# Softmax maxima transposed by VectorE instead of TensorE, first and last stages reordered, in an attention-and-experts kernel

## What is computed

```python
# attention: q from layernorm(x), k and v from the context
wq = (q @ wq_w.T + wq_b).reshape(b, t, H, DH)     # H = 16, DH = 16
wk = (k @ wk_w.T + wk_b).reshape(b, t, H, DH)
wv = (v @ wv_w.T + wv_b).reshape(b, t, H, DH)
scores = einsum('bthd,bshd->bhts', wq, wk) / sqrt(DH)
probs = softmax(scores, axis=-1)
x = x + einsum('bhts,bshd->bthd', probs, wv).reshape(b, t, d) @ wo_w.T + wo_b
# experts: xt = layernorm(x), xhat = layernorm(xt)
top1 = argmax(xt @ Wg.T, axis=-1)                 # 8 experts
for e in experts:
    h = gelu((xhat * ln_scale[e] + ln_bias[e]) @ W1[e] + b1[e])
    y += (top1 == e) * (h @ W2[e] + b2[e])
x = x + y
```

## Time and profile before

| | us |
|---|---|
| median of 3 runs | 1424.43 (1423.45 to 1425.28) |
| profiled execution, device time | 1425.39 |
| profiled execution, span from first to last instruction | 1423.6 |

### The profile page before, as it was taken

How to read it: one execution, slowest core, us unless ns; L and a number is a source line. 1 busy time by engine, 2 the same in 40 slices (tenths; PEclk the granted TensorE clock), 3 DMA queues, 4 the chain that set the end, 5 groups by cost and what they waited for, 6 DMA issues and landing times.

```text
span 1423.6 us, 40094 instructions
## 1 busy us (share of the span) xinstructions
PE 1380.6 (97%) x15314; PEld 1196.9 (84%) x15314; DVE 1158.0 (81%) x2760; ACT 985.6 (69%) x1664; POOL 482.8 (34%) x662
## 2 busy tenths in 40 slices
PE   6899999999999999999999999988999999999998
PEld 5688888888888888888888888876888888888887
DVE  4688888888888888888888888876787878878776
ACT  5477777777777777777777777756667666676764
POOL 4222332233322332233223332324444444444430
PEclk8899999999999999999999999999999999999999
DMA  6656665567656665667566755643343434434322
GB/s 183 144 146 184 171 185 150 159 172 178 161 150 175 174 176 151 167 174 182 154 159 168 185 152 154 167 114 105 91 126 106 127 105 120 117 108 132 102 80 75
DMA packets 168870, 207.46 MB, mean 146 GB/s; under 512 B 19895, under 2 KB 119530, under 8 KB 168682
## 3 DMA queue, kind: packets, MB, share of 16 engines
q1 hardware_dynamic: 168682, 204.89, 54.2%
HBM read 69.26 MB, written 33.81 MB: 72 GB/s over the span
## 4 chain that ended last, share of the span: by engine, by line
PE 88%; DVE 6%; ACT 2%; issue 2%; DMA 1%; POOL 0%; SPq 0%; ACTq 0%; DVEq 0%; POOLq 0%
PE s_ps L1345 13%; PE pp_ps L1219 11%; PE st_ps L1153 8%; PE pv_ps L1167 8%; PE s_ps L1125 8%; PE pp_ps L1192 7%; PE pp_ps L1227 6%; PE st_ps L1370 6%; PE pp_ps L1370 6%; PE pv_ps L1175 4%; PE pp_ps L1213 3%; DVE negmax L830 2%; PE pp_ps L1309 2%; PE t_ps L1144 2%; PE t_ps L1320 1%
## 5 line engine op out<-in xcount | busy, mean ns | idle before, releaser
L644 ACT ACTIVATE pT<-st_ps 128x1024 f32<-128x1024 f32 x256 | 263.1, 1028 | 108.0 <-PE st_ps L1153 107.1
L830 DVE TENSOR_REDUCE negmax<-s_ps 128x8 f32<-128x1024 f32 x256 | 311.2, 1215 | 24.3 <-PE s_ps L1125 24.0
L501 POOL TENSOR_TENSOR q_parts<-q,q_parts 128x1024 bf16<-128x1024 f32 x32 | 68.5, 2141 | 403.3 <-ACT q_parts L638 403.3
L700 ACT ACTIVATE pT<-s_ps,c 128x512 f32<-128x512 f32 x128 | 87.8, 688 | 119.4 <-PE s_ps L1345 114.3
L1125 PE MATMUL s_ps<-k_packed,q_packed 96*128 96x128 bf16 x2048 | 158.0, 220 | 11.2 <-DVE negmax L830 5.8
L1345 PE MATMUL s_ps<-k_packed,w_hi 128*128 128x512 f32 x512 | 165.8, 415 | 0.0
L1153 PE MATMUL st_ps<-q_packed,k_packed 98*128 98x128 bf16 x2048 | 158.1, 220 | 1.5 <-DMA q_packed<-negmaxT 1.5
L1125 PEld LDWEIGHTS s_ps<-k_packed,q_packed 96*128 96x128 bf16 x2048 | 128.1, 98 | 29.7 <-DVE negmax L830 17.5
L1153 PEld LDWEIGHTS st_ps<-q_packed,k_packed 98*128 98x128 bf16 x2048 | 120.6, 98 | 27.3 <-issue 25.0
L513 POOL TENSOR_TENSOR xb<-xin,bo_all 128x256 f32<-128x256 f32 x128 | 90.4, 728 | 150.8 <-DMA x_scratch<-xb 133.1
L1167 PE MATMUL pv_ps<-pT,v 128*32 128x128 f32 x4096 | 138.7, 276 | 0.0
(11 more groups left out here) (199 smaller groups left out, 3679.1 us busy)
## 6 DMA issues: line engine op xcount, KB each, us to landing
q_packed<-q_parts SPq DMA_DIRECT2D x192, 256.0 KB, 4.3
k_packed<-k_parts SPq DMA_DIRECT2D x192, 256.0 KB, 4.6
xin<-in_x_dram SPq DMA_DIRECT2D x32, 512.0 KB, 3.9
cin<-in_ctx_dram SPq DMA_DIRECT2D x32, 512.0 KB, 4.6
out_dram<-xb SPq DMA_DIRECT2D x32, 512.0 KB, 3.2
x_scratch<-xb SPq DMA_DIRECT2D x32, 256.0 KB, 4.8
x_scratch<-xb SPq DMA_DIRECT2D x64, 128.0 KB, 4.7
k_parts<-mask_scratch SPq DMA_DIRECT2D x32, 256.0 KB, 4.0
```

Of the source, the lines that this page charges most:

```text
L644: a.activation(pT[u % 2][:], st_ps[:], ACT.Exp, scale=DH ** -0.5).then_inc(s_exp, 1)
L700: a.activation(hidden32[m], h_ps[m % 2], ACT.Gelu, bias=c1[:, m:m + 1]).then_inc(f_he, 1)
L830: v.tensor_reduce(own, s_ps[:].rearrange("p (h s) -> p h s", s=P), AX_X, ALU.max, negate=True).then_inc(s_red, 1)
```

## The change

**Maxima.** `turn_max` on PE, `keep_max` on ACT and the widened tiles go. Their place takes one DVE instruction a batch, `v.transpose` of the 128x32 bf16 tile of high and low parts, which transposes each 32x32 square by itself. It waits for the low part to be complete, and stands in `maxima` of the batch's second unit. What was one 32x128 tile is now four 32x32 squares, one on each 32 partitions, so `load_max` issues four DMAs of 2 KB for a batch. Before, it was one of 8 KB.

**Start.** PE runs 80 products of a tile of ones before the first weights; VectorE makes that tile, which GpSimd made before. Group 0 is packed in two halves of two batches, 24 DMAs in place of 12, and the first scores wait for the first half alone. The products for the experts' bias move behind `scores(0, 2)`; scores of units 0 to 2 move ahead, between the first items of group 1; statistics of group 2, batch 0, move into group 0; `load_x(2)` moves behind the first `load_max`.

**Last attention group and first experts.** Groups 0 and 3 of the experts are normalised by ACT or at another place; group 0's moves from DVE (unit 1) to ACT (units 1 and 2). GpSimd computes the shift for every group. PE's first experts' group is reordered: `hidden(0, 2)` earlier, `gate(1)` and `turn_logits(1)` later, behind parts of `outputs`. DVE's order follows.

```diff
-        negmax_wide = [sb(f"negmax_wide{n}", [P, P], BF16) for n in range(2)]
-        negmaxT = [sb(f"negmaxT{n}", [2 * H, P], BF16) for n in range(2)]
+        negmax_hl = [sb(f"negmax_hl{n}", [P, 2 * H], BF16) for n in range(2)]
+        negmaxT = [sb(f"negmaxT{n}", [P, 2 * H], BF16) for n in range(2)]
...
+            def pack_half(z, part, half):
+                tok = slice(half * 2 * T, (half + 1) * 2 * T)
...
             def load_max(n, b):
-                sp.wait_ge(s_mte, at(PAIRS, n, b + 1))
-                sp.dma_start(packed[0][n % 2][KP:KP + 2, :, b * T:(b + 1) * T], negmaxT[b % 2][:]).then_inc(ld_mx[b % 2], 16)
+                sp.wait_ge(s_mt, at(PAIRS, n, b + 1))
+                for q in range(P // (2 * H)):
+                    strip = slice(q * 2 * H, (q + 1) * 2 * H)
+                    sp.dma_start(packed[0][n % 2][KP:KP + 2, :, b * T + q * 2 * H:b * T + (q + 1) * 2 * H],
+                                 negmaxT[b % 2][strip, :]).then_inc(ld_mx[b % 2], 16)
...
-            for part in range(3):
-                for z in range(2):
-                    pack(0, z, part)
+            for half in range(2):
+                for part in range(3):
+                    for z in range(2):
+                        pack_half(z, part, half)
+            load_max(0, 0)
             load_x(2)
-            load_max(0, 0)
...
-            def keep_max(n, b):
-
-                act.wait_ge(s_mt, at(PAIRS, n, b + 1))
-                wait(act, ld_mx[b % 2], 16 * at(PAIRS // 2, n, b // 2))
-                a.copy(negmaxT[b % 2][:], maxT_ps).then_inc(s_mte, 1)
...
+                    if not more and u in (1, 2):
+                        ffn_normalise_by_shift(0, range((u - 1) * 2, u * 2))
...
                 v.tensor_tensor(lo, own, hi, ALU.subtract).then_inc(s_mp, 1)
+                if m == C - 1:
+                    dve.wait_ge(s_mp, at(UNITS, n, u + 1))
+                    wait(dve, ld_mx[b % 2], 64 * at(PAIRS // 2, n, b // 2))
+                    v.transpose(negmaxT[b % 2][:], negmax_hl[b % 2][:]).then_inc(s_mt, 1)
...
-                    if not more and u == 1:
-
-                        dve.wait_ge(s_pp, ITEMS * (GROUPS - 1) + 2)
-                        ffn_normalise(dve, 0)
...
-            def turn_max(n, b):
-                pe.wait_ge(s_mp, at(UNITS, n, C * (b + 1)))
-
-                wait(pe, s_mte, at(PAIRS, n, b))
-                done = turned_at(n, C * b - 2) if b > 0 else turned_at(n - 1, UNITS - 2)
-                if done:
-                    pe.wait_ge(s_ate, at(GB, *done) + 1)
-                t.transpose(maxT_wide, negmax_wide[b % 2][:], ident_bf[:]).then_inc(s_mt, 1)
...
+            pe.wait_ge(s_ones, 1)
+            for k in range(WARM):
+                t.matmul(pv_ps[:, 0:P], ones_bf[:], ones_bf[:], start=True, stop=True)
             pe.wait_ge(s_pc, 5)
...
-            for k in range(4):
-                item(1, k)
+            item(1, 0)
+            item(1, 1)
+            pe.wait_ge(s_pad, 16 * 2)
+            scores(0, 0)
+            item(1, 2)
+            item(1, 3)
+            scores(0, 1)
+            item(1, 4)
+            scores(0, 2)
             pe.wait_ge(s_w1, 16 * 2)
...
-            scores(0, 0)
-            item(1, 4)
-            scores(0, 1)
             item(1, 5)
-            pe.wait_ge(s_wide, 2)
-            turn_max(0, 0)
-            scores(0, 2)
...
-                if nxt:
-                    turn_max(nxt[0], nxt[1] // 2)
                 if kept:
                     turn_pv(*kept)
...
             def first_ffn_group():
-                hidden(0, 2)
                 mask(2)
-                gate(1)
                 hidden(0, 3)
                 mask(3)
+                gate(1)
+                for m in range(MC - 1):
+                    outputs(0, range(2), m)
                 turn_logits(1)
```

More of the change, by code:

```diff
@@ L501, in lo, with lo_half @@
                 g.tensor_tensor(parts[z][:, 2, :, :], z32[z][:], parts[z][:, 1, :, :], ALU.subtract).then_inc(s_lo, 1)
+            def lo_half(z, half):
+                tok = slice(half * 2 * T, (half + 1) * 2 * T)
+                pool.wait_ge(s_mid, z + 1)
+                g.tensor_tensor(parts[z][:, 2, :, tok], z32[z][:, :, tok], parts[z][:, 1, :, tok],
+                                ALU.subtract).then_inc((s_lo_first, s_lo)[half], 1)
             def residual(n):
@@ L519, in _ @@
             for z in range(2):
-                lo(0, z)
+                for half in range(2):
+                    lo_half(z, half)
             g.memset(v1[1][:, :, :, DH:HP], 1.0).then_inc(s_vone, 1)
@@ L559, in ffn_norm @@
                 g.tensor_tensor(rstd[:], rstd[:], rstd2[:], ALU.mult).then_inc(f_r12, 1)
[L560 to L564, removed]
+                g.tensor_tensor(neg_mean[:], mv[:, :, 0], neg_one[:], ALU.mult).then_inc(f_nm, 1)
+                pool.wait_ge(f_r12, one)
+                pool.wait_ge(f_nm, one)
+                g.tensor_tensor(shift[:], neg_mean[:], rstd[:], ALU.mult).then_inc(f_sh, 1)
             def lo_of_xT(n):
@@ L676, in _ @@
             item(0, 9)
-            for k in range(6):
+            for k in range(4):
                 item(1, k)
-            keep_max(0, 0)
+            item(1, 4)
+            item(1, 5)
             def keep_xT(n, c):
@@ L710, in hidden_hi, with ffn_normalise_by_shift @@
                 a.copy(hT_hi[n % 2][:, m, :].bitcast(F32R), hidden32[m]).then_inc(f_hh, 1)
[L712 to L715, removed]
+            def ffn_normalise_by_shift(n, batches=range(GB)):
+                act.wait_ge(f_sh, n + 1)
+                if n == 0:
+                    act.wait_ge(s_pp, ITEMS * (GROUPS - 1) + 2)
+                wait(act, f_tr, at(C, n - 1, C))
+                for b in batches:
                     a.activation(xn[:, b, :], xf[n % XF][:, b, :], ACT.Identity, bias=shift[:, b:b + 1],
@@ L999, in _ @@
             v.tensor_copy(bo_all[:], t_ps[:, 0:D]).then_inc(s_bo, 1)
-            for k in range(3):
-                lower(1, k)
+            lower(1, 0)
+            lower(1, 1)
+            maxima(0, 0)
+            lower(1, 2)
+            maxima(0, 1)
+            lower(1, 3)
+            maxima(0, 2)
+            remainder(1, 4)
             dve.wait_ge(s_c1T, 1)
@@ L1008, in _ @@
             last.then_inc(s_c1, 1)
-            lower(1, 3)
-            maxima(0, 0)
-            remainder(1, 4)
-            maxima(0, 1)
-            maxima(0, 2)
-            stats_of(2, 0)
-            mean_of(2, 0)
             def group(n):
@@ L1090, in ffn_group @@
                     ffn_stats_of(dve, n + 3)
+                if n == 1:
+                    keep_logits(2)
                 mask_hidden(n, 0)
-                if more:
+                if 1 < n < LAST:
                     keep_logits(n + 1)
@@ L1119, in scores @@
                 tok = slice(b * T, (b + 1) * T)
-                if u == 0:
+                if n == 0 and u == 0:
+                    for z in range(2):
+                        pe.wait_ge(pk_first[z], PACK)
+                if u == (0 if n > 0 else UNITS // 2):
                     for z in range(2):
@@ L1159, in values @@
                 wait(pe, s_nrm, at(GB, n, b))
+                if n == 0 and b == 0:
+                    pe.wait_ge(s_vone, 2)
+                    pe.wait_ge(s_c1, 1)
                 if b == 0:
@@ L1428, in _ @@
             project_out(LAST, GB - 1)
+            hidden(0, 2)
             turn(1, 1)
@@ L1456, in ffn_group @@
                     turn_logits(n + 1)
+                if n == 1:
+                    hidden(n, 2)
                 if n + 2 <= LAST:
@@ L1459, in ffn_group @@
                         turn(n + 2, c)
-                hidden(n, 2)
+                if n > 1:
+                    hidden(n, 2)
                 hidden(n, 3)
```

74 lines of the change are left out of this document (40 added, 34 removed).

## The result

The changed kernel takes 1445.89 us (median, 1445.64 to 1449.25), the kernel before in the same comparison 1423.94 (1420.98 to 1425.28): a ratio of 1.0162, 95% interval 1.0148 to 1.0177, so 22 to 23 us slower. The forecast was 1443. It was near by luck: two terms of its sum were wrong by about as much in opposite directions. The experiments show which.

A forecast was written before the change was run, and what follows sets the result against it. PE and DVE in balance were taken to bound the kernel. Terms +22.2 (loops), +1.9 (last two groups), -2 (start), -1.3 and -2 (last attention group, first experts) gave +18.8, so 1443 us; range 1411 to 1462.

The forecast's parts named there:

- The bound: Attention loops: PE and DVE in balance, aT_lo ready only 0.09 and 0.06 us before use, so added DVE time lengthens loops.
- Rival (a): Attention loops: PE is the only bound and DVE has room, so removing turn_max gains 9.0 us; 1410 us, chance 0.22.
- The maxima, VectorE's side: DVE's queue behind the low part: wait 0.12 plus transpose 0.12, so 0.24 us a batch from start to start.
- the loop, both sides together: Four loops of a group lengthen by 0.20, 0.20, 0.17 and 0.17, together 0.74 us; +22.2 over 30 groups.
- The test with the cast: Earlier group with a 0.33 us cast in DVE's queue: loop 7.62 against 7.26 us, so DVE time comes out nearly fully.
- The four DMAs: SP's queue: three more issues, 2.1 us a batch, next packs up to 1 us later; cost nothing, upper end +39.
- Rival (c): The four DMAs of the maxima land late and scoresT waits in most groups: about +20, 1463 us, chance 0.13.
- Rival (d): Transpose collides with GpSimd, whose residual that step releases in one unit a group: +9, 1452 us, chance 0.10.
- rival b: A semaphore between two VectorE instructions is free, so 0.12 us a batch: about 1428 us, chance 0.10.
- Worth nothing: ACT's copy keep_max leaves, but ACT is in none of the four loops through it: 0 to -2 us.
- The ends: Start -2, last attention group's normalisation -1.3, first experts' new order -2: together -5.3 us.
- PE under 28.4 us in a group: Expected profile of the changed kernel: PE busy under 28.4 us in groups of about 29.4 us.

The follow-up runs named there:

- e3: Kernel before plus VectorE's wait and a transpose of the maxima into an unread tile, TensorE's transpose and the one DMA kept: 1437.3 us.
- e5: Kernel before plus only one more wait a batch in VectorE's queue, behind the low part of the maxima: 1429.9 us.
- e7: Changed kernel with two of the four DMAs a batch issued from ScalarE's queue instead of SyncE's: 1432.2 us.
- e4: Kernel before with the maxima of a batch sent by four DMAs in place of one, the transpose staying with TensorE: 1520.3 us.
- e9: Changed kernel with VectorE's transpose moved later in its queue, behind the attention copies, and two of the four DMAs issued by ScalarE: 1428.2 us.
- e2: Changed kernel with the maxima done as before (TensorE's transpose, ScalarE's copy, one DMA), so the new ends alone: 1421.3 us.

## Why the forecast held, and where it didn't

**The bound.** Right as a direction: VectorE stands in the loops with PE, and what is put ahead of `aT_lo` and `cT_lo` costs time. Rival (a), PE the only bound at 1410, falls by e3 and e5: they leave PE's work as it was, and cost 13.5 and 7.3 us.

**The maxima, VectorE's side.** The price of the instruction was right: 0.12 for the wait and 0.12 for the transpose were forecast from start to start, 0.12 to 0.13 and 0.14 were measured, 0.20 to 0.26 together at `aT_lo`. What failed is the step that follows, "the loop, both sides together", by which 0.74 us of it reach the end in each group. Sized by e7, where the packs are in time, the maxima cost 1432.2 - 1421.3 = 11 us (14 by the ratios), and e3, which leaves the DMAs alone, gives 13.5; the forecast had 24.1. A loop from one start of `turn_pv` to the next, medians over groups 2 to 30 in us:

| loop ending in unit | before | after | e7 | rise forecast |
|---|---|---|---|---|
| 0 | 7.28 | 7.45 | 7.46 | 0.20 |
| 2 | 7.34 | 7.46 | 7.45 | 0.20 |
| 4, low part 0.17 us | 6.48 (25 groups) | 6.41 (7) | 6.57 (28) | 0.17 |
| 4, low part over 0.3 us | 6.67 (4) | 6.92 (22) | 6.89 (1) | |
| 6 | 7.53 | 7.67 | 7.65 | 0.17 |

The loop of unit 0 rises nearly as forecast, that of unit 2 by half, and that of unit 4 hardly or not at all where nothing collides. Without the collision the four together rise by 0.36 us in the kernel after and by 0.50 in e7, not by 0.74. I had read the loop of unit 4 in one group, in which the low part took 0.60 us (the line at 589.59 above): its slack of zero was that collision's doing. In the kernel before only 4 of 29 groups have one there. In the others VectorE has room in that loop. A slack read off one group was taken for that of all 30. The test with the cast was sound but was one of the loop of unit 0 (7.62 against 7.26), just the loop in which nearly all of it comes out.

**The four DMAs.** Priced at nothing, with an upper end of 39 us; this is the step that was wrong in kind. The sum looked at the readers of the four DMAs (`scoresT`), and these were in time, as the sum said: 4.3 us in four places in the whole run. It named the packs that wait behind them in the queue, had them "up to 1 us later", and didn't ask how long before their reader they land. That could have been read in the trace of before: in 16 of 31 groups the first scores were already waiting for them or started at their landing, so there was no room for a pack that comes later. In the kernel after it is 0.59 us at 840.96. e7 prices the four issues at 13.7 us, by PE's waits about half of it packs and somewhat less the collision with GpSimd; e4 shows that the same issues can cost 96, far over the upper end.

So 24.1 was 11 to 14 and 0 was 12 to 14. That their sum, 24.7, is that of the forecast is luck. Rival (c) named the right resource and the wrong reader: its sign, `scoresT` waiting in most groups, is missing. Rival (d) was half right. What collides is the low part, as at 762.03, and not the transpose (210 to 215 ns in all 128 places), and the trace names the DMA of `x_scratch` as what releases `residual`, not the maxima's step. 18 groups have the wait for `aT_lo`, at 0.3 us or so each. As shares of the kernel they aren't apart: a group with the collision is late by it, and then its packs are nearly in time (603.23 starts unit 6 after 6.76 us, with 0.12 us of "issue"), a group without it waits for the packs.

**The semaphore** (rival b): fell with e5.

**ScalarE.** "Worth nothing" for `keep_max` has nothing against it in the kernel after; no run tests it alone. e9 shows how near ScalarE is to the bound: two issues in its place, behind a later transpose, and it is the one that PE waits for.

**The ends.** Forecast -5.3, measured -2.5 twice. In e2 the loads of the fourth group are issued at 74.62 us, before at 76.91: -2.3 for the start, where -2 was forecast. The first `scoresT` of e2 is 4.1 us earlier than in the earlier trace rows (in the kernel after, at 45.76, it is 4.6), where "near 48" stood:

```profile
46.22 1.03 PE L1186 MATMUL st_ps<-q_packed,k_packed 98*128 98x128 bf16 x8 [3.01 <-DMA q_packed<-negmaxT]
```

A third of this is given back at once. PE stood idle for 3.01 us, and behind that the granted clock was 0.50 (1.2 GHz):

```profile
46.20:50.00 3.80, 3.78 (x17) 2.88 (x18) 3.10 (x8) 2.00 (x3) 0.67 (x1) 0.50 0.93 299
```

The eight products take 1.03 us, where those at 50.34 in the earlier trace rows took 0.62 at the full clock, and from this `scoresT` to the next it is 4.48 us against 3.14 before (46.22 to 50.70, and 50.34 to 53.48). The forecast had left open whether the clock stays up at the start.

From the last group's load of the context to the end, the profiled execution of e2 is 2.0 us shorter than that of before, where 3.3 was forecast. The two profiled executions differ by 5.5 us and the medians by 2.5; the medians decide, so these two parts are upper ends.

**PE under 28.4 us in a group** was forecast and is wrong: 28.96 and 28.71. PE's busy time didn't fall by the transposes taken away, in part because the stretches begin and end at other pieces (18 of `turn_pv` in the first, not 16); the rest I can't explain. It was a bad test.

**A slip in the sum.** With 0.4 in place of 0.24 the forecast's own terms give 1.38 x 30 + 3.2 = 44.6, not 42. Nothing rests on it.

## What to carry to other kernels

An issue costs the queue its 0.6 us whether it carries 8 KB or 2 KB, so splitting a transfer is a price for everything behind it in that queue; ask of each of those when it lands and when its reader comes, not only of the transfer that is split. Where a group repeats 30 times, read the slack in several groups, and look in each for an instruction that took longer than its like; one collision makes a loop look tight that isn't. A forecast that meets the time hasn't shown its terms: take each alone, and in pairs, since here the same edit cost 5 us or gave 4 depending on who issued the DMAs.

## What the runs showed of the hardware

- Behind VectorE's subtraction of 8 elements a partition (0.17 us) the next instruction started 0.08 us after its start without a wait, and 0.20 to 0.21 with a wait for it; 128 such waits cost 7.3 us of the kernel (e5).
- The 128x32 bf16 transpose in squares took 210 to 215 ns in all 128 places, with its follower 0.14 behind its start in nearly all.
- That 0.17 us subtraction took 0.58 to 0.72 us in 23 places of the kernel after, and 2.00 us in one at the start (48.90), and each time ended 0.03 us behind the end of a GpSimd addition (128x256, or 128x1024 from 48.70 to 50.86).
- SyncE's issue of 2 KB took 607 ns in the median of the kernel after and 654 in e7, one of 8 KB 655.
- 80 products of ones raised PE's busy time in the first 10 us from 2.51 to 7.94, with no gain at the end. The granted clock from 10 to 20 us was 0.63 to 0.74 in seven profiles with them; in six without, 1.00 four times and 0.72 and 0.75.
- Behind 3.01 us without work PE's granted clock was 0.50 from 46.2 to 50.0 us in e2, and eight products took 1.03 us in place of 0.62.
